# The last 65 tokens of every batch projected together, with key groups spread evenly over the slots

## What is computed

```python
q = layernorm(x) @ Wq.T + bq
k = ctx @ Wk.T + bk
v = ctx @ Wv.T + bv
scores = einsum('bhqd,bhkd->bhqk', q, k) / sqrt(32)     # 16 heads of 32
s = where(scores >= 0, scores + 1, 1 / (1 - scores))
context = einsum('bhqk,bhkd->bhqd', s / s.sum(-1), v)
x = x + context @ Wo.T + bo
```

## Time and profile before

| | us |
|---|---|
| median of 3 runs | 1272.34 (1272.29 to 1272.39) |
| profiled execution, its own time | 1272.52 |
| its span, first to last instruction | 1270.8 |
| TensorE busy | 1260.8 (99%) |
| VectorE busy | 649.4 (51%) |
| ScalarE busy | 634.2 (50%) |
| GpSimd busy | 437.4 (34%) |

### The profile page before, as it was taken

One profiled execution on the slowest core, in us unless ns is written; L12 is line 12 of the kernel. 1 busy time (PEld: TensorE's weight loads), 2 busy tenths in 40 slices (PEclk: granted clock), 3 DMA queues, 4 the chain that ended last, 5 costly groups with the idle time before them and its releaser, 6 DMA issues.

```text
span 1270.8 us, 29915 instructions
## 1 busy us (share of the span) xinstructions
PE 1260.8 (99%) x13126; PEld 1097.3 (86%) x13126; DVE 649.4 (51%) x936; ACT 634.2 (50%) x1085; POOL 437.4 (34%) x203
## 2 busy tenths in 40 slices
PE   9999999999999999999999999999999999999998
PEld 8888888888788888888789789798989999999997
DVE  5333453444463363463354454766776555565655
ACT  4445454464545544545444646646544443554443
POOL 1445345544555545545546535200032000100000
PEclk9999999999999999999999999999999999999999
DMA  6131011021011012012012111764556499999990
GB/s 244 50 103 51 18 56 50 23 68 67 19 64 68 18 56 101 19 64 68 18 51 105 51 56 43 284 255 157 179 195 224 148 348 365 340 344 347 357 396 35
DMA packets 32775, 174.89 MB, mean 138 GB/s; under 512 B 5944, under 2 KB 8152, under 8 KB 14464
## 3 DMA queue, kind: packets, MB, share of 16 engines
q1 hardware_dynamic: 30896, 168.16, 36.0%
q0 software_dynamic: 1744, 4.76, 1.2%
HBM read 166.84 MB, written 6.06 MB: 136 GB/s over the span
## 4 chain that ended last, share of the span: by engine, by line
PE 98%; DVE 1%; DMA 0%; ACT 0%; issue 0%; DVEq 0%; SPq 0%
PE bank L740 23%; PE bank L728 22%; PE bank L1079 11%; PE sc L1096 9%; PE sc L756 8%; PE sc L941 7%; PE bank L769 4%; PE sc L960 3%; PE bank L960 3%; PE bank L833 1%; PE bank L796 1%; PE bank L887 1%; PE bank L898 1%; PE sc L898 1%; DMA ctxt<-in_ctx 0%; PE sc L999 0%
## 5 line engine op out<-in xcount | busy, mean ns | idle before, releaser
L587 POOL TENSOR_TENSOR xn<-xn,tt 128x1024 f32<-128x1024 f32 x96 | 230.1, 2397 | 330.9 <-DVE tt L1325 329.7
L1208 ACT ACTIVATE tt<-sc 128x512 f32<-128x512 f32 (+1 forms) x208 | 107.8, 602 | 351.5 <-PE sc L756 351.4
L1423 DVE TENSOR_TENSOR wsl<-ring,wsh 128x2048 fp32r<-128x2048 f32 x72 | 166.8, 2316 | 111.0 <-ACT wsh L1163 107.9
L1312 DVE TENSOR_SCALAR kk<-bank,bkt 128x512 f32<-128x512 f32 (+2 forms) x130 | 80.8, 622 | 213.6 <-PE bank L728 213.2
L728 PE MATMUL bank<-cxh,wkh 128*128 128x512 f32 (+2 forms) x512 | 181.1, 354 | 1.5 <-DVE va L1320 1.0
L728 PE MATMUL bank<-cxl,wkh 128*128 128x512 f32 (+2 forms) x512 | 174.6, 341 | 0.0
L728 PE MATMUL bank<-cxh,wkl 128*128 128x512 f32 (+2 forms) x512 | 174.1, 340 | 0.0
L740 PE MATMUL bank<-wvh,cxh 128*128 128x512 f32 (+1 forms) x416 | 163.5, 393 | 0.0
L740 PE MATMUL bank<-wvl,cxh 128*128 128x512 f32 (+1 forms) x416 | 162.7, 391 | 0.0
L740 PE MATMUL bank<-wvh,cxl 128*128 128x512 f32 (+1 forms) x416 | 162.2, 390 | 0.0
L1163 ACT CAST wsh<-ring 128x2048 fp32r<-128x2048 f32 x72 | 137.4, 1909 | 48.0 <-PE sc L1096 20.9
(11 more groups left out here) (270 smaller groups left out, 2024.2 us busy)
## 6 DMA issues: line engine op xcount, KB each, us to landing
ring<-in_w SPq DMA_DIRECT2D x112, 1024.0 KB, 6.1
ctxt<-in_ctx SPq DMA_DIRECT2D x15, 1024.0 KB, 4.9
ctxt<-in_ctx SPq DMA_DIRECT2D x8, 642.0 KB, 3.9
ctxt<-in_ctx SPq DMA_DIRECT2D x10, 512.0 KB, 3.6
wqt<-in_wo SPq DMA_DIRECT2D x4, 1024.0 KB, 4.8
wqt<-in_aq SPq DMA_DIRECT2D x4, 1024.0 KB, 5.3
wqt<-in_ap_ SPq DMA_DIRECT2D x4, 1024.0 KB, 6.9
yrows<-K SPq DMA_DIRECT2D x1, 2048.0 KB, 9.1
```

The lines of the kernel that those rows point to most:

```text
L587: e.tensor_tensor(dacc[0:kn, y, :], dacc[0:kn, y, :], tt[0:kn, w, :], ALU.add).then_inc(s["da_pool"], 1)
L1423: e.tensor_tensor(wsl[m % 3][:], ring[slot(unit_split(m))][:], wsh[m % 3][:].bitcast(F32), ALU.subtract).then_inc(s["wl_dve"], 1)
```

## The change

- The last 65 tokens of all 8 batches are loaded at the start (`tails`, 520 columns) and projected at once: keys in 96 matmuls of 260 columns (`tail_keys`), values in five groups of 12 (`tail_values`: four of two batches' 64 tokens each, one of the eight 65th tokens).
- Both are stored to DRAM (`ktail`, `vtail`). A batch's share is loaded back by `load_tail(b)`: keys into `ktb` (two buffers), values into the ring `va`.
- A batch now has three parts of 512 tokens, 24 parts in all. Key groups come one per slot at r = 0 to 11. There is none at r = 12, and no values at r = 10 and at the very last chunk's slot. The next batch's first keys are formed at r = 8 to 11.
- The queries are made of three fp32r products of 512 columns (48 matmuls) in place of 32 fp32 matmuls of 256 columns; the split of their weights and rows adds work on ScalarE, VectorE and GpSimd.
- Some tiles of the expert stage get another place in memory, and the scratch for indirect DMAs is set to 4096 bytes.

```diff
-SPANS = ((0, 512), (512, 512), (1024, 256), (1280, 321))
+TAIL = 65
+NPART = 3 * NB
...
 def first(i):
-    b, (k0, n) = PARTS[i]
-    return PER * b + k0 // P
+    return PER * (i // 3) + 4 * (i % 3)
...
 def key_groups(slot):
-    early, late = [], []
+    groups = []
     for i in range(1, NPART):
         f = first(i - 1)
...
+        groups += [(i, slot - f)] * (0 <= slot - f < 4)
+    return groups
...
 def values_in(slot):
     if slot + 2 < NCH - 3:
-        return slot + 2
-    return slot if NCH - 3 <= slot < NCH else None
+        return None if is_tail(slot + 2) else slot + 2
+    return slot if NCH - 3 <= slot < NCH - 1 else None
...
+            def load_tail(b):
+                if b >= 2:
+                    e.wait_ge(s["s_pe"], PER * (b - 1))
+                e.dma_start(ktb[:, b % 2, :, :].rearrange("p g n -> p (g n)"),
+                            ktail[:, 4 * TAIL * b:4 * TAIL * (b + 1)]).then_inc(s["kt_in"], 16)
+                n = PER * b + PER - 1
+                e.wait_ge(s["p_pe"], n - VR + 1)
+                e.dma_start(va[0:TAIL, n % VR, :], vtail[b]).then_inc(s["vt_in"], 16)
...
                 for i in range(3, NPART):
                     if first(i - 2) - 2 == n:
-                        e.wait_ge(s["cl_pool"], i - 1)
+                        e.wait_ge(s["cl_pool"], i)
                         load_ctx(i)
+                if n % PER == PER - 2:
+                    load_tail(n // PER)
...
             def scores(n):
...
+                if is_tail(n):
+                    e.wait_ge(s["kt_in"], 16 * (b + 1))
                 for g in range(4):
-                    if k == 0:
+                    if k == 0 and not is_tail(n):
                         e.wait_ge(s["proj_read"], use["k", i, g] + 1)
...
             def weighted(n):
...
-                e.wait_ge(s["proj_read"], use["v", n] + 1)
+                if tail:
+                    e.wait_ge(s["vt_in"], 16 * (b + 1))
+                else:
+                    e.wait_ge(s["proj_read"], use["v", n] + 1)
```

More of the change, by code:

```diff
@@ L45, in first, with is_tail, tokens, place @@
 def first(i):
-    b, (k0, n) = PARTS[i]
-    return PER * b + k0 // P
[L51 to L63, removed]
+    return PER * (i // 3) + 4 * (i % 3)
+def is_tail(n):
+    return n % PER == PER - 1
+def tokens(n):
+    return TAIL if is_tail(n) else P
+def place(n):
+    b, j = divmod(n, PER)
+    return 3 * b + j // 4, j % 4
+def formed(n):
+    return (PER - 1) * (n // PER) + n % PER
 def key_groups(slot):
-    early, late = [], []
+    groups = []
     for i in range(1, NPART):
         f = first(i - 1)
[L71 to L79, removed]
+        groups += [(i, slot - f)] * (0 <= slot - f < 4)
+    return groups
 def ending(slot, lag):
@@ new lines, in tail_values @@
+            def tail_values(j):
+                dst, kn = take("vt", j), (8 if j == 4 else P)
+                col = 260 * (j // 2) + P * (j % 2)
+                if j < 2:
+                    e.wait_ge(s["kt_dve"], 8 + 2 * j + 2)
+                if j == 4:
+                    e.wait_ge(s["tl_dve"], 3)
+                for c in range(4):
+                    if j == 0 and c % 2 == 0:
+                        e.wait_ge(s["wvl_dve"], c // 2 + 1)
+                    for x_, (a, b) in enumerate(three):
+                        m = e.matmul(dst[0:kn, :], (ceh, cel)[a][:, c, :] if j == 4 else
+                                     (cxh, cxl)[a][:, 1, c, col:col + P], (wvh, wvl)[b][:, c, :],
+                                     start=(c == 0 and x_ == 0), stop=(c == 3 and x_ == 2))
+                m.then_inc(s["vt_pe"], 1)
@@ L732, in values @@
             def values(n):
[L733 to L737, removed]
+                i, k = place(n)
+                u, dst = i % 2, take("v", n)
                 for c in range(4):
                     for x_, (a, b) in enumerate(three):
-                        m = e.matmul(dst[0:kn, :], (cxh, cxl)[a][:, u, c, k * P:k * P + kn], (wvh, wvl)[b][:, c, :],
+                        m = e.matmul(dst[:], (cxh, cxl)[a][:, u, c, k * P:k * P + P], (wvh, wvl)[b][:, c, :],
                                      start=(c == 0 and x_ == 0), stop=(c == 3 and x_ == 2))
@@ L744, in scores @@
             def scores(n):
-                i, k, kn = chunk(n)
-                u, b, c0 = i % 2, n // PER, 256 * (n - group_of(n)[0])
+                i, k = place(n)
+                b, c0, kn = n // PER, 256 * (n - group_of(n)[0]), tokens(n)
                 if n >= 2:
@@ L1201, in act @@
                 for m in group(n):
-                    kn = chunk(m)[2]
+                    kn = tokens(m)
                     if m >= TR:
@@ L1502, in vector @@
             e.tensor_copy(kio[:], iotai[:, P:P + 120].rearrange("p (k e) -> p k e", e=8)).then_inc(s["iota_dve"], 1)
-            values(0)
-            values(1)
+            for g in range(4):
+                keys(0, g)
+            for n in range(2):
+                values(n)
             count = [0]
@@ L1651, in vector @@
                     weights(m, 1)
-                for i, g in late:
-                    keys(i, g)
                 for b, g, m in finished(n)[1]:
```

368 lines of the change are left out of this document (230 added, 138 removed).

## The result

| | before | after |
|---|---|---|
| median, us | 1272.32 | **1379.2** (1378.64 to 1379.38, 4 runs) |
| ratio | | **1.084** [1.082, 1.086] |
| profiled span, us | 1270.8 | 1376.8 |
| TensorE busy, us | 1260.8 | 1277.0 |

A forecast was written before the change was run, and what follows sets the result against it. TensorE, busy 99% of the span, was taken as the bound. -15.7 + 0.2 + 6.3 + 2.8 + 2.3 = -4.1, plus 7 x (11.3 + 2.3) = 95.2, gave +91.1 on 1272.5: 1363 us, range 1330 to 1385.

The forecast's parts named there:

- The added wait: TensorE at r = 12, batches 0 to 6, idles 11.3 us for the tail's keys, queued behind a context load.
- The first rival: The tail's keys overtake the context load, wait 8.4 us, total 1330 to 1343; chance 0.15.
- The clock after each wait: After each of seven waits TensorE restarts at half speed, costing 2.3 us; bounds 0.4 and 4.4.
- the tail's own chain: After the tail's scores, ScalarE and VectorE delay the next scores: 0.4 us extra wait unthrottled, included in the 2.3.
- The clock after the 6.3 us gap: Last batch, after the gap before r = 10's scores: half speed for 4.7 us, +2.3 us.
- The last batch's waits: Removed work had filled waits: +6.3 us before the scores at r = 10, +2.8 us at the last slot.
- A batch: Profile sign: each batch lasts 91.5 - 4.9 + 13.6, about 100 us.
- What is removed: TensorE work saved: keys -3.8, values -8.7, queries -3.2, together -15.7 us.
- the moved tiles ... I cost at nothing: Tiles at other places in memory, and the smaller scratch, were given no cost.
- the price of 2.75 us for a group of 12: Time per 12 TensorE matmuls of 512 columns, taken from the profile before and used for the changed kernel.
- first keys: At the start TensorE begins at the same time, since the two loads it waits for keep their old sizes.
- the forecast's -1.3: Second rival: the tail's loads come in time, no wait, 7 x 0.4 - 4.1 = -1.3, 1271 us; chance 0.05.

The follow-up runs named there:

- the shorter wait: The change with the tail's loads issued after SyncE's wait for the low context half but before the context load: 1356.18 us (1.066).
- engine kept busy: The change plus 200 unread 128x128 matmuls on TensorE before the wait for the tail's keys, batches 0 to 6: 1370.43 us (1.077).
- tail's loads first: The change with only SyncE's order altered, the tail's loads issued ahead of the same slot's context load: 1287.75 us (1.012).
- the run that kept two values late: The change with the tail's loads issued first, plus values of chunks 99 and 100 formed at r = 8 and 9 of the last batch: 1285.73 us.

## Why the prediction was right, and where it was off

- **The added wait**: right in mechanism, place and size. Forecast 11.3 us in batches 0 to 6; measured 80.0 / 7 = 11.4. Its links also held. Counted from the scores at r = 10 of batch 0, GpSimd's two sums and `context_lo`, in a row without a gap, end at 17.4 us and the keys land at 22.8 (forecast 17.4 and 22.7); TensorE is ready at 11.5 (11.4). Shown by moving the loads.
- **The first rival**, that the tail's keys overtake: not seen once in eight loads (4.9 to 5.4 us). Its price was near: issued before the context load, the load took 2.1 us (2.0 forecast) and the wait was 8.1 (8.4).
- **The clock after each wait**: forecast 2.3 us, in which 0.4 stood for the tail's own chain. The runs give 1.6 by three comparisons (with and without the wait, with the shorter wait, engine kept busy), and some 0.2 to 0.4 a batch for the chain, which the runs without the wait still have (`L830 <- DVE tt`); the pieces themselves give 2.0. The slow start lasts 2.8 to 6.0 us, 4.3 in the mean, so the 4.7 read off the program's start was a fair mean and no constant. The step was right and somewhat too large, 2 to 3 us in all.
- **The clock after the 6.3 us gap**: forecast 2.3, measured 3.6, and 4.2 with the tail's loads first (values 7.12 us there). The same row of the start was used for both; here the slow stretch was some 7 us long and reached well into the values group.
- **The last batch's waits**: 6.3 and 2.8 forecast, 6.2 and 2.2 measured. Right, and the run that kept two values late shows that refilling one gap opens another.
- **A batch**: "a batch of 91.5 - 4.9 + 13.6, about 100 us" holds for batch 1 alone, 101.1 from one tail's exponentials to the next. The 91.5 us is that batch's time before; the five after it took 97.6 to 101.1 before and take 108.3 to 112.3 now. The difference, 9.5 to 11.2, is what the sum needs, so the forecast of the total doesn't suffer.
- **What is removed**: the counts were right, and the queries take 10.94 us (forecast 11.0; the four pieces before add up to 14.05, not 14.2). A slip in the last part of the text: a batch without the wait loses 4.7 us of matmuls by the terms of the sum ((3.8 + 8.7 + 25.3) / 8), not 4.9; measured, with the wait gone, 2.8.
- **The step that failed is "the moved tiles ... I cost at nothing", and with it the price of 2.75 us for a group of 12 after the change.** The pitch of 520 columns in the context tiles isn't named in the forecast at all. The group takes 2.79. On the kernel before, the same memory costs 8.6 us with nothing else changed: 3.3 by the relative starts of the expert stage's tiles, about 5 by what remains, the pitch of 520. In the change there are 197 such groups against 164 and almost no short ones, so by the same step (5.2 / 164 = 0.03 each, 0.04 when the short groups, which gained a little, are set apart) it is some 8 us of pitch and 3.3 of starts: 11. The 3.3 were also found on the change's side, nearly (2.3, or 3.1 with the clock's 0.8); the 8 are carried over from the kernel before and were not measured on the change.

The difference of 16 us between forecast and result then reads: layout 11; clock at the end of the last batch 1.3; first keys 0.7 later (8.18 against 7.51); waits +0.9 in seven batches and -0.7 in the last; clock in seven batches -2 to -3. That sums to 11 or so; some 5 us are open, of which the tail's keys at the start are 0.4 (12.0 us against 11.6). That the range held the result thus owes something to errors of both signs, though most of the forecast is the wait, which came out within 1 us. "Tail's loads first" leaves about the same: 15.4 us less the forecast's -1.3 are 16.7, of which layout, clock, first keys and last batch explain 11 + 1.9 + 0.7 - 0.7, 13.

## What to carry to other kernels

A load that is cheap and early in its data can still be late in its queue: before moving a wait onto a DMA, write down what stands ahead of its issue, and what that waits for. Moving two lines of SyncE was worth 91.5 us here. And a change of tile shapes is a change of matmul time: compare the mean ns of an untouched group before and after, and put the new memory under the old work to price it, before explaining a residue by waits. Where a filler is put back into a gap, look at the order on the engine that must hand its result on: here VectorE's split of weights stood ahead of the copy.

## What the runs showed of the hardware

- A split (fp32r) matmul of 512 columns takes 389 to 390 ns in records and 2.72 us for twelve in one memory layout, and 393 to 395 ns and 2.78 us in another, with the same instructions. A shift of the tiles of both stages by 32 bytes, or of all tiles by 12288, does nothing; different starts modulo 2048 bytes cost 3.3 us over the expert stage (48 matmuls 11.13 us against 10.90). What remains, about 5 us of the attention (800.90 to 806.11 at the eighth tail), is put down to the pitch of 520 columns by exclusion: no run had the pitch of 512 and all else of the change.
- The matmuls of 256 columns didn't become longer with it (280 ns against 283).
- A load of 130 KB lands 2.1 us after issue alone and 4.9 to 5.4 right behind one of 1 MB in the same queue.
- After 11.4 us of idle TensorE the granted clock is 0.50 for the first 2.8 to 6.0 us of work (seven waits of one execution), which makes that work 2.0 us longer and the kernel 1.6 a wait. After 6.2 us of idle time the matmuls that follow are as slow (3.69 us for 64 against 1.94), and for some 7 us; after 3.0 us too (24 values in 6.79 to 7.73 us against 5.5).
- VectorE's split of a 128x2048 weight tile takes 4.03 us beside GpSimd's sums of 4.9 us, and 2.33 in the mean of all 72.
